# Attention's projections on fp16 halves of the normed rows, with the split in front of the turn, and later negations

## What is computed

```python
Q = _rope(x @ Wq.T + bq)
K = _rope(x @ Wk.T + bk)
V = x @ Wv.T + bv
A = jnp.einsum('btd,bsd->bts', Q, K) / jnp.sqrt(jnp.float32(C))
A = jnp.where(causal, A, -jnp.inf)
A = jax.nn.softmax(A, axis=-1)
out = jnp.einsum('bts,bsd->btd', A, V)
return out @ Wf.T + bf
```

## Time and profile before

| | |
|---|---|
| median of 3 runs | 774.8 us (773.57 to 776.81) |
| the profiled execution | 773.13 us, of which its span (first to last instruction) is 771.3 us |
| scores(0) starts | 357.69 us |
| scores(14) starts | 448.68 us |
| scores(15) starts | 455.06 us |

### The profile page before, as it was taken

How to read it: one execution, slowest core, us unless ns; L and a number is a source line. 1 busy time by engine, 2 the same in 40 slices (tenths; PEclk the granted TensorE clock), 3 DMA queues, 4 the chain that set the end, 5 groups by cost and what they waited for, 6 DMA issues and landing times.

```text
span 771.3 us, 18265 instructions
## 1 busy us (share of the span) xinstructions
PE 712.1 (92%) x6093; PEld 621.8 (81%) x6094; DVE 445.7 (58%) x1218; ACT 370.5 (48%) x871; POOL 293.1 (38%) x259
## 2 busy tenths in 40 slices
PE   5989985999999999989899999799999999999981
PEld 5768974889888897668789988688888888888871
DVE  5897678344444443437897778745454555555440
ACT  6898745433344433333667656343433444343430
POOL 3348101222333224114455430226555655564331
PEclk9999996999999999999999999899999999999996
DMA  9896998114122112137741279112333332332235
GB/s 273 189 211 81 140 165 265 43 29 120 28 41 41 27 22 35 22 67 193 151 56 18 39 94 316 32 36 43 45 51 55 43 46 48 55 48 41 36 36 154
DMA packets 42214, 66.22 MB, mean 86 GB/s; under 512 B 3680, under 2 KB 29264, under 8 KB 41616
## 3 DMA queue, kind: packets, MB, share of 16 engines
q0 software_dynamic: 22304, 39.19, 33.5%
q1 hardware_dynamic: 19664, 25.93, 10.6%
q10 hardware_dynamic: 192, 0.38, 0.1%
HBM read 65.80 MB, written 23.35 MB: 116 GB/s over the span
## 4 chain that ended last, share of the span: by engine, by line
PE 74%; DVE 13%; ACT 4%; DMA 3%; issue 2%; POOL 1%; POOLq 0%; SPq 0%; DVEq 0%
PE PS L1146 16%; PE PS L1159 15%; PE PS L853 14%; PE PS L890 8%; PE PS L1513 3%; PE PS L868 3%; PE PS L2451 3%; PE PS L2465 2%; ACT Y L2171 2%; PE PS L1540 1%; PE PS L1131 1%; PE PS L1463 1%; DMA xs<-Y 1%; DMA X<-in_w_dram 1%; PE PS L1521 1%
## 5 line engine op out<-in xcount | busy, mean ns | idle before, releaser
L1159 PE MATMUL PS<-X 128*128 x720 | 125.8, 273 | 1.9 <-ACT X L1228 1.9
L1325 POOL DMA_INDIRECT sum<-X,dest x45 | 89.7, 1993 | 96.2 <-ACT X L1228 80.5
L1146 PE MATMUL PS<-X 128*128 128x256 f16 (+1 forms) x768 | 122.7, 265 | 0.7 <-issue 0.7
L1218 ACT ACTIVATE X<-PS,X 128x256 f32<-128x256 f32 (+1 forms) x192 | 72.6, 461 | 103.5 <-PE PS L1146 100.4
L853 PE MATMUL PS<-Y,X 128*128 128x256 f16 x960 | 108.1, 273 | 0.5 <-DVE Y L1022 0.5
L853 PEld LDWEIGHTS PS<-Y,X 128*128 x960 | 93.9, 98 | 11.5 <-issue 0.7
L1146 PE MATMUL PS<-X,Y 128*128 128x256 f16 (+1 forms) x384 | 100.2, 264 | 0.0
L1159 PE MATMUL PS<-Y,X 128*128 x360 | 98.2, 273 | 0.0
L1117 POOL DMA_INDIRECT sum<-Y,dest x24 | 38.6, 1610 | 111.4 <-DVE Y L1050 107.8
L1146 PEld LDWEIGHTS PS<-X 128*128 x768 | 71.7, 97 | 10.6 <-issue 1.3
L1159 PEld LDWEIGHTS PS<-X 128*128 128x128 f16 x720 | 70.4, 98 | 11.1 <-issue 3.0
(11 more groups left out here) (408 smaller groups left out, 1385.3 us busy)
## 6 DMA issues: line engine op xcount, KB each, us to landing
X<-in_w_dram POOLq DMA_DIRECT2D x10, 1024.0 KB, 16.2
X<-in_w_dram POOLq DMA_DIRECT2D x8, 768.0 KB, 15.4
sum<-h SPq DMA_DIRECT2D x2, 2048.0 KB, 15.1
Y<-in_w_dram POOLq DMA_DIRECT2D x4, 1024.0 KB, 11.3
xs<-Y SPq DMA_DIRECT2D x2, 1040.0 KB, 6.2
xs<-Y SPq DMA_DIRECT2D x2, 1032.0 KB, 8.8
h<-in_txt_dram SPq DMA_DIRECT2D x2, 1024.0 KB, 16.5
Y<-in_patches_dram SPq DMA_DIRECT2D x3, 672.0 KB, 7.7
```

Source lines behind the costliest of these rows:

```text
L1146: ins = nc.tensor.matmul(PS[:, 2 * s + c // 2, (c % 2) * T1:(c % 2) * T1 + tokens], part[:, off:off + P], x_[:, slot, k, 0:tokens], start= ...
L1159: ins = nc.tensor.matmul(PS[:, 4 + a, 0:D], h_[:, s, c, a * P:(a + 1) * P], part[:, off:off + D], start=(s == 0 and c == 0 and n == 0), st ...
L1218: ins = nc.scalar.activation(hh1[:, s, c, 0:tokens], PS[:, 2 * s + c // 2, (c % 2) * T1:(c % 2) * T1 + tokens], ACT.Gelu, bias=bias1[:, sl ...
L1325: nc.gpsimd.indirect_dma_start(out=sum1, out_offset=bass.IndirectOffsetOnAxis(ap=dest[:, i:i + 1], axis=0), in_=y1buf[:, u % 2, i - first_ ...
```

## The change

The normed rows are split into two fp16 halves, a rounded high one and the rest, before they are turned. POOL does this for text rows (a rounding copy and a subtraction, `split_text`), DVE for image rows (`norm_image`). PE then turns four fp16 tiles where it turned two of fp32, and makes queries, keys and values as three fp16 products each (high by high, high by low, low by high) where there was one fp32 product. The weights are split once: ACT rounds Wq and Wk, DVE subtracts, POOL splits Wv (`split_values`). PE's order of steps stays; its `text` now waits for `xn_split`. POOL's `split_text(b+2)` is put between `rope(b+1)` and `image(b+2)`. The negations begin with batch 2 by a table, and the DMAs that add the weights are issued in batches 6, 9 and 12. Some semaphores of the first mixture's weights are merged to free numbers.

```diff
+NEGATED1 = (0, 0, 1, 1, 1, 1, 1, 2, 1, 1, 2, 1, 1, 2, 1, 0)
+ADD_IN = (6, 9, 12)
...
             def text(b, slot):
-                pe.wait_ge(xn_ready, NF + b + 1)
+                pe.wait_ge(xn_split, b + 1)
...
-                for k in range(KC):
-                    ins = nc.tensor.transpose(PS[:, 7, k * P:(k + 1) * P], xnF[:, slot, k * P:(k + 1) * P], k_ident)
+                for q in range(2 * KC):
+                    ins = nc.tensor.transpose(turned2[:, q * P:(q + 1) * P], xn2[:, slot, q // KC, q % KC * P:(q % KC + 1) * P],
+                                              ident2)
...
                         for k in range(KC):
-                            ins = nc.tensor.matmul(PS[:, bank, m * SEQ:(m + 1) * SEQ], w_[:, k, m * P:(m + 1) * P],
-                                                   xTb[:, slot, k, :], start=(k == 0), stop=(k == KC - 1))
+                            for n, (wh, xq) in enumerate(((0, k), (0, KC + k), (1, k))):
+                                ins = nc.tensor.matmul(PS[:, bank, m * SEQ:(m + 1) * SEQ], w_[:, wh, k, m * P:(m + 1) * P],
+                                                       xTb[:, slot, xq, :], start=(k == 0 and n == 0),
+                                                       stop=(k == KC - 1 and n == 2))
...
+            pe.wait_ge(wqk_parts, 3)
             project(0, 0)
             keep_clock(16, 5)
+            pe.wait_ge(wvx_split, 1)
             text_values(0, 0)
...
-                for n in range(b + 1 if b else 0, min(b + 2, W1W // CW)):
+                for n in range(sum(NEGATED1[0:b]), sum(NEGATED1[0:b + 1])):
...
+            def split_text(b):
+
+                pool.wait_ge(xn_ready, NF + b + 1)
+                nc.gpsimd.tensor_copy(xn2[:, b % 2, 0, :], xnF[:, b % 2, :]).then_inc(own_rounded, 1)
+                pool.wait_ge(own_rounded, b + 1 + (b > 0))
+                nc.gpsimd.tensor_tensor(xn2[:, b % 2, 1, :], xnF[:, b % 2, :], xn2[:, b % 2, 0, :], ALU.subtract)\
+                    .then_inc(xn_split, 1)
+
+            def split_values():
+
+                pool.wait_ge(wqk_parts, 3)
+                nc.gpsimd.tensor_copy(wvx2[:, 0], wvx).then_inc(own_rounded, 1)
+                pool.wait_ge(own_rounded, 2)
+                nc.gpsimd.tensor_tensor(wvx2[:, 1], wvx, wvx2[:, 0], ALU.subtract).then_inc(wvx_split, 1)
...
+            split_text(0)
             image(0)
+            pool.wait_ge(prep_copied, 4)
+            split_values()
+            split_text(1)
             image(1)
             rope(0)
-            pool.wait_ge(prep_copied, 4)
             bias(0)
             bias(1)
...
                 if b < BATCH - 1:
                     rope(b + 1)
                 if b < BATCH - 2:
+                    split_text(b + 2)
                     image(b + 2)
                     bias(b + 2)
```

More of the change, by code:

```diff
@@ L326, in build @@
         xnF = rx.take([IT + 2, D])
-        xTi = rx.take([KC, IT, P])
-        xTb = rx.take([2, KC, SEQ])
+        xTi = rx.take([2 * KC, IT, P], F16)
+        xTb = rx.take([2, 2 * KC, SEQ], F16)
         qkT = rx.take([2, 2, KC, SEQ])
@@ L342, in build @@
         rsum = rx.take([2, 2])
+        xn2, xi2 = rx.take([2, 2, D], F16), rx.take([2, 2, D], F16)
+        wqk2 = stage[:, 1, :].bitcast(F16).rearrange("p (h n) -> p h n", h=2)
+        wq2, wk2 = (wqk2[:, :, i * KC * D:(i + 1) * KC * D].rearrange("p h (k n) -> p h k n", k=KC) for i in range(2))
+        wvx2 = wqk.bitcast(F16)[:, 0:2 * KC * PAYV].rearrange("p (h k n) -> p h k n", h=2, k=KC)
+        ident2 = stage[:, 0, CW - P // 2:CW].bitcast(F16)
+        turned2 = PS[:, 7, :].bitcast(F16)
         rg = Region(X, XE)
@@ L395, in build @@
         d_moved = sem("d_moved")
-        w0_cast = [sem(f"w0_cast{i}") for i in range(W0C // CAST)]
+        w0_cast = [sem(f"w0_cast{i}") for i in range(4)]
         own_negated = sem("own_negated")
@@ L492, in build @@
         p_exp = sem("p_exp")
+        own_rounded = sem("own_rounded")
+        xn_split = sem("xn_split")
+        wqk_parts = sem("wqk_parts")
+        wvx_split = sem("wvx_split")
         p_normed = sem("p_normed")
@@ L1520, in text_values @@
                 for k in range(KC):
-                    ins = nc.tensor.matmul(PS[:, 2, 0:PAYV], xTb[:, slot, k, IMG:SEQ], wvx[:, k, :],
-                                           start=(k == 0), stop=(k == KC - 1))
+                    for n, (xq, wh) in enumerate(((k, 0), (k, 1), (KC + k, 0))):
+                        ins = nc.tensor.matmul(PS[:, 2, 0:PAYV], xTb[:, slot, xq, IMG:SEQ], wvx2[:, wh, k, :],
+                                               start=(k == 0 and n == 0), stop=(k == KC - 1 and n == 2))
                 ins.then_inc(v_psum, 1)
@@ L1531, in image_values @@
                 for k in range(KC):
-                    ins = nc.tensor.matmul(PS[:, 5, 0:PAYV], xTi[:, k, n, :], wvx[:, k, :], start=(k == 0), stop=(k == KC - 1))
+                    for j, (xq, wh) in enumerate(((k, 0), (k, 1), (KC + k, 0))):
+                        ins = nc.tensor.matmul(PS[:, 5, 0:PAYV], xTi[:, xq, n, :], wvx2[:, wh, k, :],
+                                               start=(k == 0 and j == 0), stop=(k == KC - 1 and j == 2))
                 ins.then_inc(vi_psum, 1)
@@ L1702, in negate @@
                         .then_inc(w1_negated, 1)
+            act.wait_ge(attn_loaded, 96)
+            nc.scalar.activation(wqk2[:, 0, :], wqk, ACT.Copy).then_inc(wqk_parts, 1)
+            nc.scalar.activation(ident2, k_ident, ACT.Copy).then_inc(wqk_parts, 1)
             act.wait_ge(prep_psum, 3)
@@ L1804, in pool_attention @@
                     image_bias(IMAGE_BIAS.index(b))
-                if b and b % (W1N // CW) == 0:
-                    add(b * CW // W1N - 1)
+                if b in ADD_IN:
+                    add(ADD_IN.index(b))
             add(E1 - 1)
```

44 lines of the change are left out of this document (26 added, 18 removed).

## The result

| | kernel before | changed kernel |
|---|---|---|
| median | 774.48 us (773.57 to 776.81, 4 runs) | 817.25 us (815.93 to 818.86, 4 runs) |
| ratio | | 1.0555, 95% interval 1.0537 to 1.0574 |
| profiled execution | 773.13 us, span 771.3 us | 815.93 us, span 814.1 us |
| scores(0), scores(14), scores(15) start | 357.69, 448.68, 455.06 us | 361.84, 491.23, 497.80 us |

The changed kernel is 5.5% slower. 820 us was predicted, with 799 to 835 as the range, so time and direction came out as forecast. The sum behind them was right in its shape and wrong in some of its terms, and part of the closeness is luck, since the errors have both signs.

What follows compares the result with a forecast made beforehand. PE's work and a ring through PE, DVE and POOL were taken to bound the loop nearly equally. 773.1 + 27.4 (loop) + 2 (start) - 0.7 (last turn) + 17 (clock) = 818.8, median 820 us, range 799 to 835.

Steps and rivals of the forecast that it cites:

- The sum: Whole kernel: profiled 773.1 us, +27.4 loop, +2 before scores(0), -0.7 to scores(15), +17 clock falls, giving 818.8.
- the loop without the clock: Attention loop, scores(0) to scores(14), without clock falls: 118.4 us against 91.0, so +27.4.
- the clock: PE's granted clock falls in each of 14 attention-loop turns, at 1.2 us a fall: +17 us.
- the start: Ahead of scores(0): POOL's added splits and image copies delay rope(0), so scores(0) comes 2 us later.
- the last turn: From scores(14) to scores(15): no text in it, shorter by the query half, about -0.7 us.
- The added wait: Attention loop: PE's text(b+2) waits for POOL's split behind rope(b+1), pushing transpose_p, text_values and scores behind it.
- The idle stretch: PE, from the end of values at 2.15 us into a turn to about 6.0: 3.8 us idle every turn.
- The length of the turn: One attention-loop turn from project's start: 8.2 us against 5.99, with POOL's split taken at 1.5.
- The rival of the held clock: Attention loop: the same longer turns but no falls of PE's clock, 803 us; chance 0.18.
- what I costed at nothing: ACT's longer copy, DVE's image-tile instructions, ACT's and DVE's weight split, later weight DMAs, second negations, merged semaphores: 0 us.
- The split is in time: Rival: POOL's split ends before PE reaches text(b+2), so turns take 5.62 us and the kernel 768; chance 0.05.
- the ring: Attention loop: project on PE, DVE's multiplications, POOL's additions, scores on PE; 5.99 us a turn before the change.

Runs made afterwards that it cites:

- the filled kernel: The changed kernel with 40 further fp16 matmuls of unused result on PE ahead of text(b+2) in batches 0 to 13: 802.08 us, ratio 1.0363.
- the last experiment: The changed kernel with one more POOL subtraction (128 x 528) between the rounding copy and the subtraction of Wv's split, ahead of the loop: 821.8 us, one run.
- repaired version: The changed kernel with text norm and split one batch ahead (774.97 us); plus weight issues, image splits and filler moved or added (773.5); plus DVE, ACT, POOL reordering (771.32).

## Why the prediction held, point by point

**The sum.** For the profiled execution 818.8 was predicted and 815.93 came. The terms are off by -1.9 (the loop without the clock), -4.1 (the clock), +1.0 (the start), +0.9 (the last turn) and +1.2 (layer 0, which no term foresaw). They come to -2.9 together only because they have both signs; by size they add up to 9.1. That much of the closeness is luck.

**The added wait.** Right, and it decided: text waits for L1802 14 times, and moving the split ahead takes the loss away.

**The idle stretch.** 3.8 us in every turn were predicted, 2.4 to 2.9 came in 12 of the 14. Apart from the split, which was shorter than taken, a reading was wrong: PE's end of values was put at 1.71 + 0.44 = 2.15 into the turn, but values has two steps, and 0.44 is the second one alone. PE's timeline of the kernel before, ahead of the earlier trace rows:

```profile
425.28 2.49 PE L1513 MATMUL PS<-X,Y 128*128 128x165 f32 x16
427.61 0.60 PE L1562 MATMUL PS<-X 128*128 128x260 f32 x2
```

The first step runs from 427.61 to the second at 428.05. In the changed kernel values ended at 403.22, 2.83 into the turn. The fall in every turn was argued from 3.8 us and lost that ground.

**The length of the turn.** 8.2 us were predicted, 7.87 came. The step that failed is the price of the split: 1.5 was chosen, the rows show 404.90 to 406.04, 1.14. Two smaller errors nearly cancel. The stretch from project to the split took 4.51 and not 4.37, as the 425.44 that it was counted from is a start in the chain, and project itself starts at 425.28. For PE's 0.17 behind the split, and the 0.1 of POOL's wait on itself, no row was given; 0.06 and 0.08 came. The groups of POOL's instructions by form, changed kernel, 361 to 498 us (busy us, mean ns):

```profile
L1802 POOL TENSOR_TENSOR X<-X 128x256 f16<-128x256 f32 x14 | 9.4, 668 | 1.1
L1800 POOL CAST X<-X 128x256 f16<-128x256 f32 x14 | 5.5, 395 | 0.0
```

The cast took 0.395, just what lay between the two copies of the earlier trace rows; the far row of 0.927, which pulled my choice up to 0.6, was no guide. The Trainium skill ("GPSIMD Engine Reference", section "Engine selection": one-input operations roughly at line rate) had it at that cheap end, and the trace is near it here: DVE's cast of the same form took 0.29. The subtraction, 0.668, was also below the nearest row (0.727), so the true price lay just under my low bound of 1.2. The fp16 durations held: project 1.74 (1.71 expected), text_values 0.68.

**The loop without the clock.** 118.4 was predicted, 116.5 is what the filled kernel shows. Two errors nearly cancel: 14 x 0.33 = 4.6 too much for the turn, and 2.7 not priced (116.5 - 14 x 7.87 - 3.6). Of these, 1.2 lie in the third turn, where DVE's first statistics and an image tile delay the rope and hence the split (5.74 us from project to the split, 4.51 in an undisturbed turn). Another 0.7 lie in the ninth and 0.35 in the twelfth, and each follows a batch with two negations on ACT. In the ninth the filled kernel's chain of waits runs through them, and from there through the exponentials to DVE's rope and the split; in the twelfth DVE waits 0.25 us for the exponentials in the middle of the rope's products. The chain's piece in the ninth (start us, us):

```profile
429.51 1.89 ACT Y L1728 x2
```

I had listed both at nothing, DVE's added instructions and the second negation of a batch.

**The clock.** The mechanism was right and the price of one fall too (1.2 taken, 1.4 measured; 1.6 by the same working for the 11 falls of the last experiment), but not the count: nine and not 14, so 12.9 us instead of 17. Waits of the same length sometimes left the clock alone. The rival of the held clock, 803 us, is what the filled kernel reached (802), with the same errors of the turn inside.

**The start.** 2 us predicted, 2.95 came, and by another way. POOL's list, which I added up, had 2.2 us idle in it. DVE was the bound: it splits the two image tiles ahead of rope(0), 0.8 each (1.11 us from a tile's norm to what follows its split, where 0.32 lay before), and stood 1.2 us still beside POOL's split of Wv (0.54 - 0.18 and 1.05 - 0.18). Within 0.1 these are the 2.7 us by which the way from the first image tile's norm to rope(0) grew (7.50 against 4.76). The splits of the image tiles stood among what I costed at nothing, with 0.8 each if their cover were gone, and at the start it was gone. None of the rows read from the kernel before shows such a stall.

**The last turn.** -0.7 predicted, +0.2 came: scores(14) and the start of project ran in the last low stretch of the clock (2.01 us for scores instead of 1.09). In the filled kernel, with no low stretch there, it took 5.90, 0.5 less than before.

**The rivals.** "The split is in time" was put at 768 us and the turn at 5.62. With the split really in time the turn was 5.65. But that kernel took 775, and its loop 90.3 us where the rival had 82: a fall of the clock made the second turn 2.5 longer, and DVE became the bound in turns with statistics, for which the rival allowed 3 us.

## What to carry to other kernels

A shorter product is no gain where the work that prepares it is put on the ring that sets the pace. Ask first which engine's list the new instruction stands in, what it stands behind, and what on the busiest engine waits for it: here 1.14 us on POOL moved 1.2 us of PE's filling work out of a gap and made the loop 38 us longer, and with the same instructions one batch earlier it took 90.3 us, against 91.0 before and 88.9 with the negations alone. Try the parts of a mixed change apart: the reordered negations were a gain of 2.3 us that the sum did not show. And when an engine is relieved, look for the next one; in each repaired version the longest turns were those with DVE's statistics.

## What the runs showed of the hardware

- A DVE instruction can stand still for as long as a POOL instruction runs: 0.17 to 0.18 us became 0.54, 0.58, 0.92, 1.04 and 1.05, each time to within 0.05 us of the end of POOL's. Not every one does: the rope's products, which read PSUM, took 0.38 and 0.37 at 359.86 and 360.16 in the changed kernel, beside POOL's addition from 359.73 to 360.62. It goes the other way too: POOL's cast of 256 columns, 0.40 in the loop, took 0.67 from 358.04 on, behind a DVE subtraction that ran from 358.03 to 358.46. The Trainium skill ("SBUF — State Buffer", section "Who interferes with whom") tells of a pair of ports that the two engines share; beside a DVE instruction in a two-port mode, whichever starts first holds the pair until it ends. The trace agrees where DVE's instruction began behind POOL's (354.03 behind 353.92, 354.82 behind 354.62); in which mode DVE's instructions ran it does not show. By that rule the 1.2 us of these two would have stood in the term of the start.
- Most of the low clock lay on work and not on the idle time ahead of it: 12.9 us lost of the 16 that the 32 us at half clock ahead of scores(14) can cost at most. 40 small matmuls a turn in the gap gave 15 us back in the medians, 11.4 in the loop of the two profiled executions.
- What decides whether a wait of 2.4 to 2.9 us brings a fall is left open: the changed kernel had both in one execution.
